# Where the two scans of an RWKV layer stand in VectorE's and ScalarE's order

## The reference

```python
h = layernorm(x, ln1_w[l], ln1_b[l]); hh = time_shift(h)
k  = (h * tmk[l] + hh * (1 - tmk[l])) @ Wk[l].T
v  = (h * tmv[l] + hh * (1 - tmv[l])) @ Wv[l].T
sr = sigmoid((h * tmr[l] + hh * (1 - tmr[l])) @ Wr[l].T)
x  = x + (sr * wkv(time_decay[l], time_first[l], k, v)) @ Wo[l].T
...                                    # second half: another layernorm, Wck (relu, square), Wcv, Wcr
def step(carry, kv):                   # wkv, one step in time
    aa, bb, pp = carry
    ...
    out = (e1 * aa + e2 * vv) / (e1 * bb + e2)
    return ((e1b * aa + e2b * vv, e1b * bb + e2b, qq2), out)
```

## Time and profile before

| | us |
|---|---|
| median of 4 runs (lowest to highest) | 6156.05 (6152.8 to 6167.61) |
| profiled execution | 6157.9 |
| its span on core 5, the slowest | 6156.3 |
| PE busy | 4080.0 (66%) |
| DVE busy | 2787.3 (45%) |
| ACT busy | 2050.5 (33%) |
| POOL busy | 966.2 (16%) |

### The profile page before, as it was taken

One profiled execution on the slowest core, in us unless ns is written; L12 is line 12 of the kernel. 1 busy time (PEld: TensorE's weight loads), 2 busy tenths in 40 slices (PEclk: granted clock), 3 DMA queues, 4 the chain that ended last, 5 costly groups with the idle time before them and its releaser, 6 DMA issues.

```text
span 6156.3 us, 63786 instructions; the slowest of 8 cores (6129.0 to 6156.3 us)
## 1 busy us (share of the span) xinstructions
PE 4080.0 (66%) x18700; PEld 1914.3 (31%) x18700; DVE 2787.3 (45%) x4164; ACT 2050.5 (33%) x3003; POOL 966.2 (16%) x1332
## 2 busy tenths in 40 slices
PE   2245359577585967758577685876958769587455
PEld 0022124233242423324233342432424324243222
DVE  3463064453536435363553535435354353452554
ACT  3333033324233342323334243342433424323221
POOL 2322322222222222222222000000000000000000
PEclk6567679798897978879798897987979879798777
DMA  5355557566675767657575341423414324244233
GB/s 175 115 158 179 160 176 244 168 223 199 190 227 170 239 181 216 198 186 237 167 232 186 116 134 65 144 91 101 140 65 137 99 92 151 65 137 132 79 123 105
DMA packets 410478, 954.68 MB, mean 155 GB/s; under 512 B 31936, under 2 KB 42384, under 8 KB 410144
## 3 DMA queue, kind: packets, MB, share of 16 engines
q1 hardware_dynamic: 299344, 576.98, 29.9%
q0 software_dynamic: 100400, 355.26, 17.8%
q10 hardware_dynamic: 10400, 18.35, 0.9%
HBM read 825.95 MB, written 124.52 MB: 154 GB/s over the span
## 4 chain that ended last, share of the span: by engine, by line
DMA 39%; PE 26%; POOL 11%; DVE 11%; issue 9%; ACT 3%; DVEq 0%; POOLq 0%; SPq 0%; ACTq 0%
DMA wstage<-wsrc 38%; PE bank L417 22%; POOL wconv L329 8%; POOL wcache L333 3%; PE bank L463 2%; DVE bpool L609 2%; DVE sdf L687 1%; DVE snf L677 1%; DMA wring<-wcache 1%; ACT bpool L447 1%; DVE snf L537 1%; DVE snf L532 1%; ACT h L576 1%; DVE rwkv L742 1%; PE bank L507 1%
## 5 line engine op out<-in xcount | busy, mean ns | idle before, releaser
L417 PE MATMUL bank<-bpool,wring 128*128 128x448 bf16 x12480 | 2589.5, 370 | 1070.8 <-DVE bpool L609 647.7
L417 PEld LDWEIGHTS bank<-bpool,wring 128*128 128x128 bf16 x12480 | 1247.5, 101 | 2430.9 <-issue 1410.6
L329 POOL CAST wconv<-wstage 128x1024 bf16<-128x1024 f32 x440 | 489.6, 1113 | 2175.1 <-DMA wstage<-wsrc 2175.1
L609 DVE SCALAR_TENSOR_TENSOR bpool<-dsq,cvb,h 128x448 bf16<-128x448 bf16 x880 | 631.9, 722 | 89.0 <-DVE dsq L598 3.3
L417 PE MATMUL bank<-rwkv,wring 128*128 128x448 bf16 x1280 | 288.1, 393 | 332.7 <-DVE rwkv L742 332.7
L841 DVE TENSOR_TENSOR sdf<-rwkv,bank 128x448 f32<-128x448 bf16 x160 | 99.4, 621 | 879.7 <-PE bank L417 879.7
L463 PE MATMUL bank<-bpool,ones 128*1 128x448 bf16 x440 | 172.6, 573 | 422.7 <-ACT bpool L447 422.7
L983 POOL DMA_DIRECT2D out<-xres x5 | 4.3, 852 | 2747.0 <-issue 2391.8
L585 DVE COPY bcol<-h 128x8 bf16<-128x8 bf16 x45 | 8.6, 190 | 910.4 <-ACT h L576 909.9
L632 ACT ACT_TABLE_LOAD x19 | 24.4, 1283 | 1158.8 <-PE bank L417 1158.8
L447 ACT ACTIVATE bpool<-xres 128x3584 bf16<-128x3584 f32 x55 | 175.0, 3182 | 559.0 <-DVE xres L757 329.0
(11 more groups left out here) (79 smaller groups left out, 4146.4 us busy)
## 6 DMA issues: line engine op xcount, KB each, us to landing
wring<-wcache SPq DMA_DIRECT2D x1100, 512.0 KB, 4.6
wstage<-wsrc POOLq DMA_DIRECT2D x440, 512.0 KB, 5.0
wcache<-wconv POOLq DMA_DIRECT2D x440, 256.0 KB, 2.5
xres<-x ACTq DMA_DIRECT2D x5, 1792.0 KB, 25.7
snf<-x ACTq DMA_DIRECT2D x5, 1792.0 KB, 9.8
out<-xres POOLq DMA_DIRECT2D x5, 1792.0 KB, 6.8
cvs<-cvec SPq DMA_DIRECT2D x1, 192.0 KB, 2.7
```

Source lines behind the costliest of these rows:

```text
L329: ev_cvt = bld.op("gps", lambda q, s=s: q.tensor_copy(wconv[:, s, :], wstage[:, s, :]), deps=cdeps)
L417: last = q.matmul(banks.t[bank][:, 0:w], ap, moving_fn(j), start=(j == 0), stop=(j == nacc - 1))
L609: q.scalar_tensor_tensor(bp(base, c), dsq[:, c, :], cvb[:, row, c:c + 1], h[:, c, 0:ts], ALU.mult, ALU.add),
```

## The change

The denominator's half of the wkv computation is moved out of the v loop. The two state copies stand ahead of the k loop. The denominator's scan and its addition follow the two exponentials of their chunk inside the k loop. All eight pairs of Ln and Exp follow in a loop of their own, ahead of the v loop. The multiplication of numerator and reciprocal moves from the r loop into the v loop. No instruction is added or taken away, and PE's order is the same.

```diff
         def attn_tau(l, tau):
             t0 = tau * ts
             pump(3)
+            rc_evs = [None] * NCH
+            e_ci = bld.op("dve", lambda q: q.tensor_copy(
+                snf[:, :, 0:1],
...
+            e_cj = bld.op("dve", lambda q: q.tensor_copy(
+                sdf[:, :, 0:1],
...
             for p in range(NCH):
                 bk, dk = banks.acquire(pin=True)
...
+                e_sd = bld.op("dve", lambda q, p=p, lam_b=lam_b:
+                              q.tensor_tensor_scan(
+                                  sdf[:, p, 1:ts + 1], lam_b,
+                                  ekf[:, p, :], sdf[:, p, 0:1],
+                                  ALU.mult, ALU.add),
+                              deps=[e_ek, e_cj] + ev_lam_all
+                              + R_sd.rd_deps())
+                R_sd.did_write(e_sd)
+                R_lam.did_read(e_sd)
+                R_ek.did_read(e_sd)
+                e_den = bld.op("dve", lambda q, p=p: q.tensor_tensor(
+                    sdf[:, p, 0:ts], sdf[:, p, 0:ts],
+                    bp(XB0, p), ALU.add),
+                    deps=[e_sd, e_eku] + R_bp["xb"].rd_deps()
+                    + R_state.rd_deps())
+                R_bp["xb"].did_read(e_den)
+                R_sd.did_write(e_den)
+            for p in range(NCH):
+                e_l1 = bld.op("act", lambda q, p=p: q.activation(
+                    sdf[:, p, 0:ts], sdf[:, p, 0:ts], AF.Ln),
+                    deps=R_sd.rd_deps() + R_sd.wr_deps())
+                R_sd.did_write(e_l1)
+                e_rc = bld.op("act", lambda q, p=p: q.activation(
+                    sdf[:, p, 0:ts], sdf[:, p, 0:ts], AF.Exp,
+                    scale=-1.0), deps=[e_l1])
+                R_sd.did_write(e_rc)
+                rc_evs[p] = e_rc
             for p in range(NCH):
                 bv, dv = banks.acquire()
...
-                e_sd = bld.op("dve", lambda q, p=p, lam_b=lam_b:
-                              q.tensor_tensor_scan(
-                                  sdf[:, p, 1:ts + 1], lam_b,
...
                 e_num = bld.op("dve", lambda q, p=p: q.tensor_tensor(
                     snf[:, p, 0:ts], snf[:, p, 0:ts],
                     dsq[:, p, :], ALU.add),
-                    deps=[e_sd] + R_dsq.rd_deps() + R_state.rd_deps())
+                    deps=[e_sn, e_ekuv] + R_dsq.rd_deps()
+                    + R_state.rd_deps())
...
-                e_den = bld.op("dve", lambda q, p=p: q.tensor_tensor(
...
-                e_l1 = bld.op("act", lambda q, p=p: q.activation(
...
-                e_rc = bld.op("act", lambda q, p=p: q.activation(
...
+                e_wkv = bld.op("dve", lambda q, p=p: q.tensor_tensor(
+                    snf[:, p, 0:ts], snf[:, p, 0:ts],
+                    sdf[:, p, 0:ts], ALU.mult),
+                    deps=[e_num, rc_evs[p]] + R_sd.rd_deps())
+                R_sn.did_write(e_wkv)
+                R_sd.did_read(e_wkv)
...
-                e_wkv = bld.op("dve", lambda q, p=p: q.tensor_tensor(
...
                 e_rw = bld.op("dve", lambda q, p=p: q.tensor_tensor(
                     rwkv[:, p, :], snf[:, p, 0:ts], srf[:, p, :], ALU.mult),
-                    deps=[e_wkv, e_sr] + R_rwkv.rd_deps()
+                    deps=[e_sr] + R_sn.wr_deps() + R_rwkv.rd_deps()
                     + R_rwkv.wr_deps())
```

More of the change, by code:

```diff
@@ L625, in attn_tau @@
             pump(3)
+            rc_evs = [None] * NCH
+            e_ci = bld.op("dve", lambda q: q.tensor_copy(
+                snf[:, :, 0:1],
+                snst[:].rearrange("p (c o) -> p c o", o=1)),
+                deps=R_state.rd_deps() + R_sn.wr_deps())
+            R_sn.did_write(e_ci)
+            R_state.did_read(e_ci)
+            e_cj = bld.op("dve", lambda q: q.tensor_copy(
+                sdf[:, :, 0:1],
+                sdst[:].rearrange("p (c o) -> p c o", o=1)),
+                deps=[e_ci] + R_sd.wr_deps())
+            R_sd.did_write(e_cj)
+            R_state.did_read(e_cj)
             for p in range(NCH):
@@ L643, in attn_tau @@
                 R_bp["xb"].did_write(e_eku)
[L644 to L655, removed]
+                lam_b = lam[:, l, p:p + 1].broadcast_to([128, ts])
+                e_sd = bld.op("dve", lambda q, p=p, lam_b=lam_b:
[25 more added lines that the diff above has]
+                rc_evs[p] = e_rc
             for p in range(NCH):
@@ L680, in attn_tau @@
                                   ALU.mult, ALU.add),
-                              deps=[e_ekv, e_cj] + ev_lam_all
+                              deps=[e_ekv, e_ci] + ev_lam_all
                               + R_sn.rd_deps())
@@ L696, in attn_tau @@
                     dsq[:, p, :], ALU.add),
-                    deps=[e_sd] + R_dsq.rd_deps() + R_state.rd_deps())
+                    deps=[e_sn, e_ekuv] + R_dsq.rd_deps()
+                    + R_state.rd_deps())
                 R_dsq.did_read(e_num)
                 R_sn.did_write(e_num)
-                e_den = bld.op("dve", lambda q, p=p: q.tensor_tensor(
[L701 to L705, removed]
-                e_l1 = bld.op("act", lambda q, p=p: q.activation(
-                    sdf[:, p, 0:ts], sdf[:, p, 0:ts], AF.Ln),
-                    deps=[e_den] + R_sd.rd_deps())
-                R_sd.did_write(e_l1)
-                e_rc = bld.op("act", lambda q, p=p: q.activation(
-                    sdf[:, p, 0:ts], sdf[:, p, 0:ts], AF.Exp,
-                    scale=-1.0), deps=[e_l1])
-                R_sd.did_write(e_rc)
+                e_wkv = bld.op("dve", lambda q, p=p: q.tensor_tensor(
[4 more added lines that the diff above has]
+                R_sd.did_read(e_wkv)
             e_si = bld.op("dve", lambda q: q.tensor_copy(
```

## The result

| | before | after |
|---|---|---|
| ratio of the times, 95% interval | | 1.0218 [1.0202, 1.0235] |
| executions that count | 6152.8 to 6167.61 us | 6279.49 to 6299.12 us |
| steady span, median | 6143.8 us | 6281.0 us |

The change makes the kernel 2.2% slower, 134 us on 6156. In many executions of either kernel one die of four cores ran at a lower granted clock and took some per cent longer, so that plain medians over all executions come out the other way round (6376.81 us before, 6299.12 after); the ratio leaves these executions out, and the "steady span", by which I go where few executions are left, is the longest span among the four cores of each die that kept its clock.

The account below looks back on a forecast made before the run. Converted weights bound the first pass, a DVE compute chain ahead of Wo passes 2 to 20. Nineteen passes at 7.2 us less 4 us give 133 us more, 6289 against 6156; range 6250 to 6320.

Parts of the forecast that it names:

- Nothing behind Wo has slack: After the Wo projection starts: PE waits there each pass, so the full 7.2 us delay counts in nineteen passes, 137 us.
- the sum: Whole kernel: nineteen passes at 7.2 us, 137, less 4 us back from conversion; 133 us slower, 6289 against 6156.
- scan and addition, per pair: Denominator in the k loop: each chunk's scan waits for the previous chunk's addition, so a pair takes 2.03 us.
- The stall: Ahead of chunk 0's L722 in the v loop: DVE waits for all eight Exps, idle 7.9 us per pass.
- The product's move: Multiplication by the reciprocal, from r loop to v loop: free where it was, costs 0.73 us per chunk where it goes.
- the right ring: In the r loop: each sigmoid waits for the previous chunk's product L742, 1.49 us per chunk before and after.
- The hole: Ahead of the v loop, before the change: DVE waits 5.78 us for the first v projection; the moved denominator fills it.
- The step from the copies to the first L749: From the state copies through k loop, Ln/Exp and v loop to the first r-loop product: 53.8 us.
- The first pass: Pass one of twenty: its 7.2 us delay vanishes in PE's 21.7 us wait for weights, so it costs nothing.
- Rival 1: In the v loop: chunk 0's L722 does not wait for all eight Exps; 12 us less, 6144; chance 0.07.
- Rival 2: First 3400 us: weights bound it, ten passes absorb their delay and nine pay, 65 us, 6221; chance 0.04.
- Rival 3: In the r loop: products run at DVE's 0.73 us instead of 1.49; 36 us slower in all, 6192; chance 0.03.

Follow-up runs that it names:

- exp_by_chunk: The changed kernel with product L722 waiting only for its own chunk's Exp, not every write to sdf; ratio to before 1.0046, steady span 6141.9 us.
- srf_by_chunk: The changed kernel with each r-loop sigmoid no longer waiting for the previous chunk's product; ratio to before 1.0065, steady span 6178.6 us.
- before_srf: The kernel before the change, its sigmoids no longer waiting for the previous chunk's product; ratio 0.997, steady span 6133.9 us against 6140.5.
- the pipelined kernel: Changed kernel, L722 back in the r loop, waits by chunk in three loops, no DVE instruction following one it needs; ratio 0.9586, steady span 5857.3 us.

## Why the prediction was right, and the step of it that failed

The forecast was 6289 us; 6156.05 times 1.0218 is 6290. The mechanism in the attention part was right. What failed is the step "Nothing behind Wo has slack": of the delay at Wo, 13 us come back behind it, where the sum had 4. That the total still met the time to 1 us is in part luck. The steps up to Wo, in us from the start of the second state copy (4198.29 in the rows of before, 4274.71 here):

| step | predicted | measured, core 3, pass 15 |
|---|---|---|
| scan and addition, per pair | 2.03 | 2.02 |
| first Ln starts | 16.5 | 16.37 |
| idle in front of L722 | 7.9 | 8.02 |
| v loop, per chunk | 3.60 | 3.59 |
| first L749 starts | 53.8 | 53.35 |
| L749 to L749 | 1.49 | 1.49 |
| last L749 ends | 64.8 | 64.40 |

**The stall** is what exp_by_chunk took away, 139 us; 19 x 7.9 = 150 would have been the sum. The waits of L722 are 160.6 us in 20 passes, where I had 150.

**The product's move** was priced with the right ring: srf_by_chunk and before_srf show both halves of the argument. The prediction did not say that DVE's own pair of products was just as long, 0.73 + 0.76 = 1.49 us; the product was free in the old r loop, but nothing was to spare beside it.

**The hole.** The prediction calls the 5.78 us in front of the v loop the one hole of the stretch. Its own rows show two more, 1.43 us in front of L720 and 0.95 in front of the first L742. The sum of the parts doesn't suffer, since the steps after the change were added up one by one.

**The step from the copies to the first L749** was 0.43 us too long: 0.16 up to the first L722, 0.10 in the v loop and 0.17 behind the last L722. There I took the second copy's successor at 0.27 as at L720 to L735, but L749 does not depend on that copy and starts 0.10 behind it (4327.96 to 4328.06). On core 3 PE starts Wo 65.0 us behind the copies in the mean of the nine late passes, against 58.0 before: a delay of 7.0 us and not 7.2.

**The first pass** costs little, as said. PE's wait for weights, 21.74 us on core 5 before, is 14.54 on core 3 now:

```profile
602.85 3.14 PE L417 MATMUL bank<-bpool,wring 128*128 128x448 bf16 x8 [14.54 <-DMA wring<-wcache]
```

The second pass begins at 774 us in the mean of cores 0 to 3, against 771 before, where the eight cores lie up to 17 us apart.

**The sum: the failed step.** Cores 0 to 3 can be held against each other, before and after. Their spans differ by 125 us in the mean (6261 against 6136), not by 133:

| us, mean of cores 0 to 3 | in the sum | measured |
|---|---|---|
| first pass | 0 | 2.7 |
| passes 2 to 11, up to the last product | 72 | 71.5 |
| passes 2 to 11, behind it | -4 | -6.6 |
| passes 12 to 19, up to the last product | 57.6 | 56.6 |
| passes 12 to 19, behind it | 0 | -3.2 |
| last pass, up to the last product | 7.2 | 6.8 |
| what follows it | 0 | -3.2 |

The rows up to the last product are met. The prediction gave the stretch behind Wo no slack, "since PE waits there in each pass", and let only 4 us come back, by way of the conversion. Measured are 13: 6.6 in passes 2 to 11, where the conversion runs, and 6.4 behind it, where the sum had nothing. Cores differ from one another in these rows by several us, so that each is uncertain by 2 to 3 us, and 13 against 4 stands at about twice its uncertainty: the step failed as far as one pair of executions can tell, and its size is not sharp. In passes 2 to 11 PE's waits for `wring` are 4 us shorter (46.9 against 50.7 us). What gives the rest back stays open.

The 125 us come from one execution of each kernel, and the one after the change was short: the mean over the four cores of a steady die is 6269.0 us in all executions together, 8 above this one. The ratio's interval, 124 to 145 us, holds both 125 and 133. So the time of 6290 neither bears out the 4 us in the sum nor speaks against it; what speaks against it is the traces.

A pass in passes 2 to 11 takes 271.1 us on core 3, where I had 274: the 266.7 from which I started was a long one, the mean of these ten was 264.8.

**Rival 1** (no stall, a faster kernel) described what the event list in the code seems to ask for, and exp_by_chunk shows what that kernel would have given: 0.7 to 1.0 us per pass in front of Wo, as priced, but 2 us in the steady span and 7 in the mean of the cores, where I had 12. **Rival 2** is out, since passes 2 to 11 are longer by nearly as much as the later ones: 6.5 us each against 6.7, in the mean of cores 0 to 3. **Rival 3** is out, since the products stand 1.49 us apart.

## What to carry to other kernels

Where dependences are kept by whole buffer, moving an instruction moves its waits too: a list of events per chunk is worth nothing while the buffer's newest write stands beside it, and a reader moved into another loop chains that loop's writers to it. Before moving work out of a loop, find out whether it is on that loop's ring or beside it; here the product was free in one loop and cost 0.73 us per chunk, and a stall of 8 us, in the other. Where a VectorE instruction followed the one it waits for, another chunk's instruction put between them brought the step from 0.73 to 0.54 us here. And when a forecast meets the time, hold the terms of its sum against the trace all the same: here one was a third of what was measured.

## What the runs showed of the hardware

- A VectorE instruction of 0.62 us starts 0.54 us behind an independent one and 0.73 behind one that it waits for; behind a scan of 1.15 us it is 1.06 (the pipelined kernel) against 1.25. With an order that avoids all such neighbours, and waits by chunk, the stretch from the copies to the last product shrank from 57.6 to 43.0 us, 2 us more than I had worked out.
- The granted clock in a window where PE did nothing was 0.50 before and 0.71 after, with an idle stretch of 15.0 and 12.6 us. The groups that followed ran at 0.89 and 0.91. In the mean over passes 12 to 19 and the cores, the 64 matmuls of Wo take 14.3 us from the first to the last in both kernels, so the shorter idle stretch bought nothing there.
